# State-space decays through DRAM and GpSimd, unread bf16 products on TensorE, experts by pairs: one change to a twelve-stage kernel

## What is computed

```python
z, xs, Braw, Craw, dt_raw = split(layernorm(x) @ W_in)      # 512, 512, 64, 64, 64
dt = softplus(dt_raw + dt_bias)                             # 64 heads
a = exp(-exp(A_log) * dt)
Bh, Ch = rms(Braw) + B_bias, rms(Craw) + C_bias             # per head
phi = cumsum(dt, over tokens)[..., None] * rope_freqs
Bh, Ch = rope(Bh, phi), rope(Ch, phi)                       # r1 = v1*cos - v2*sin, r2 = v1*sin + v2*cos
h_t = a_t * h_(t-1) + (xs_t * dt_t) outer Bh_t ;  y_t = h_t . Ch_t
y = y / 8 + D_param * xs ;  g = y * silu(z) ;  x += (rms(g) * norm_w) @ W_out
```

## Time and profile before

| | us |
|---|---|
| median of three runs | 3548.45 (3546.27 to 3550.61) |
| the profiled execution | 3546.08 |
| its span, first to last instruction | 3543.8 |
| TensorE, matmul busy | 2886.8 (81%) |
| DVE busy | 2235.7 (63%) |
| ACT busy | 1481.2 (42%) |
| POOL busy | 628.6 (18%) |
| mean granted TensorE clock | 0.879 of 2.4 GHz |
| state-space stage, its first to its last instruction | 1030.7 to 1520.0 |
| expert stage | 2083 to 2307.5 |

### The profile page before, as it was taken

One profiled execution on the slowest core, in us unless ns is written; L12 is line 12 of the kernel. 1 busy time (PEld: TensorE's weight loads), 2 busy tenths in 40 slices (PEclk: granted clock), 3 DMA queues, 4 the chain that ended last, 5 costly groups with the idle time before them and its releaser, 6 DMA issues. The chain is left out here.

```text
span 3543.8 us, 63690 instructions
## 1 busy us (share of the span) xinstructions
PE 2886.8 (81%) x24052; PEld 2012.8 (57%) x24052; DVE 2235.7 (63%) x4757; ACT 1481.2 (42%) x3064; POOL 628.6 (18%) x990
## 2 busy tenths in 40 slices
PE   6777699977767878848996958979999996888687
PEld 3333488867645555525664434536565565777576
DVE  6999644432658888866655733257777774433764
ACT  4899511111454646343442122245555541332222
POOL 5222100000002222111110014112222212322100
PEclk8899799989977776769998978989999997999798
DMA  4999900000010000010001050000000003000000
GB/s 122 199 204 205 225 4 0 0 24 3 17 54 3 3 2 3 2 73 10 6 12 50 23 143 24 0 7 4 3 3 3 3 3 148 1 1 1 1 1 13
DMA packets 316791, 141.92 MB, mean 40 GB/s; under 512 B 296251, under 2 KB 306107, under 8 KB 312897
## 3 DMA queue, kind: packets, MB, share of 16 engines
q1 hardware_dynamic: 308356, 138.85, 16.4%
q10 hardware_dynamic: 8256, 0.52, 0.2%
HBM read 68.04 MB, written 3.15 MB: 20 GB/s over the span
## 5 line engine op out<-in xcount | busy, mean ns | idle before, releaser
L1251 ACT ACTIVATE l0x_pb<-l0x_ex,l0x_neg_max,l0x_q_scale 128x2048 uint16<-128x2048 f32 x128 | 267.2, 2088 | 35.3 <-POOL l0x_neg_max L1354 24.8
L1150 PE MATMUL l0x_s_ps<-l0x_kT,l0x_qT 128*128 128x512 bf16 x512 | 178.3, 440 | 78.8 <-DVE l0x_ex L1449 42.1
L1447 DVE TENSOR_SCALAR_CACHE_REDUCE l0x_ex<-l0x_s_ps 128x1024 f32<-128x1024 f32 x128 | 156.1, 1220 | 13.6 <-PE l0x_s_ps L1150 12.8
L1449 DVE TENSOR_SCALAR_CACHE_REDUCE l0x_ex<-l0x_s_ps 128x1024 f32<-128x1024 f32 x128 | 156.1, 1219 | 1.0 <-PE l0x_s_ps L1150 1.0
L1150 PEld LDWEIGHTS l0x_s_ps<-l0x_kT,l0x_qT 128*128 128x128 bf16 x512 | 33.5, 101 | 157.7 <-DVE l0x_ex L1449 106.3
L264 PE MATMUL l3x_bank<-l3x_w_kv_x,l3x_ctxT 128*128 128x512 f32 x256 | 117.4, 601 | 4.4 <-ACT l3x_ctx_q L765 3.7
L2230 PE MATMUL l1a_bank<-l1a_r,l1a_r 32*64 32x64 f32 x2048 | 73.1, 285 | 44.6 <-DVE l1a_r L2572 40.1
L2238 PEld LDWEIGHTS l1a_bank<-l1a_u,l1a_gm 64*64 64x64 f32 x2048 | 97.7, 197 | 17.8 <-issue 17.0
L2238 PE MATMUL l1a_bank<-l1a_u,l1a_gm 64*64 64x8 f32 x2048 | 100.4, 237 | 7.5 <-DVE l1a_gm L2591 7.3
L264 PE MATMUL l2f_bank<-l2f_w,l2f_ln_yT 128*128 128x352 f32 x256 | 105.6, 548 | 0.0
L1160 PEld LDWEIGHTS l0x_o_ps<-l0x_v,l0x_vT 128*128 128x128 f16 x2048 | 71.6, 99 | 56.5 <-DMA l0x_vT<-l0x_pb 26.7
(11 more groups left out here) (775 smaller groups left out, 7690.5 us busy)
## 6 DMA issues: line engine op xcount, KB each, us to landing
l2f_wproj_raw<-in_L_xattn_wproj SPq DMA_DIRECT2D x2, 2048.0 KB, 13.4
l3a_w<-in_L_attn_W SPq DMA_DIRECT2D x4, 1024.0 KB, 11.8
l2f_w<-in_L_ffn_w SPq DMA_DIRECT2D x1, 2816.0 KB, 10.7
l0x_ex<-in_ctxT SPq DMA_DIRECT2D x8, 256.0 KB, 5.3
l0a_wq<-in_L_attn_W_Q SPq DMA_DIRECT2D x1, 2048.0 KB, 11.4
l0a_wk<-in_L_attn_W_K SPq DMA_DIRECT2D x1, 2048.0 KB, 14.2
l0x_vT<-l0x_pb SPq DMA_TRANSPOSE x128, 4.7
l0a_wv<-in_L_attn_W_V SPq DMA_DIRECT2D x1, 2048.0 KB, 8.0
```

What stands on the lines that cost most here:

```text
L1150: ins = mm(s_ps[:, j * 512:(j + 1) * 512], qT[:, h, :], kT[:, h // 2, j * 512:(j + 1) * 512], start=True, stop=True)
L1251: s.activation(pb[:, h % 4, :], ex[:, h % 4, :], ACT.Exp, scale=q_scale[:, h:h + 1], bias=nb[:, h:h + 1], accum_out=sums[:, h:h + 1]).then ...
L1447: v.tensor_scalar(ex[:, h % 4, 0:1024], s_ps[:, 0:1024], 1.0, None, ALU.mult, ALU.max, accum_out=low_max[:, h:h + 1]).then_inc(o.up(scores ...
L1449: v.tensor_scalar(ex[:, h % 4, 1024:2048], s_ps[:, 1024:2048], 1.0, None, ALU.mult, ALU.max, accum_out=high_max[:, h:h + 1]).then_inc(o.up ...
```

## The change

In `l1_attn` the `differences` of TensorE, both kinds of steps and `dta` go. The running sum times `-exp(A_log)` is taken by ACT from the PSUM bank (`cum_a`, heads on partitions), stored to DRAM by SP and read back eight times per tile with the source repeated over 64 partitions, straight into `decay`. TensorE transposes `cum_a` to tokens on partitions (`cum_s`). POOL subtracts and adds the mask, for 16 heads at a time; ACT's exponential then works in place. `biased_b` is POOL's alone, in halves; `biased_c` and `sines` go by halves. `keep_warm` issues bf16 products of 128 x 512 whose result nobody reads. Per tile there are 22 while the next half is turned, 16 in `group_scores`, 11 in `mix`. In `Moe` two experts (2 x 176 = 352 = 128 + 128 + 96 columns) share three transposes, three products and two copies.

```diff
 class Moe:
-        self.parts = [(a, min(P, inner - a)) for a in range(0, inner, P)]
+        self.parts = [(a, min(P, 2 * inner - a)) for a in range(0, 2 * inner, P)]
...
-            if 1 <= i <= E:
+            if i >= 2 and i % 2 == 0:
...
-            if i >= 2:
+            if i >= 3 and i % 2:
...
+                s.activation(flat(self.actT[:, pair % 2, 0:whole_rows, :]), self.tb[:, 0:whole_rows * P], ACT.Copy)
@@ l1_attn, sync
+            for t in range(TILES):
+                sp.wait_ge(cum_a_ready.sem, cum_a_ready.value(t))
+                sp.dma_start(cum_dram[t].rearrange("b h s -> h b s"), cum_a[0:H, :].rearrange("h (b s) -> h b s", b=2)).then_inc(cum_stored.sem, 16)
+                sp.wait_ge(cum_stored.sem, cum_stored.value(t))
+                for r in range(4):
+                    if t and r % 2 == 0:
+                        sp.wait_ge(gm_ready.sem, gm_ready.value(t - 1, r // 2 + 1))
+                    for b in range(2):
+                        src = cum_dram[t, b, 16 * r:16 * r + 16, :].unsqueeze(0).broadcast_to([S, 16, S])
+                        sp.dma_start(decay[b * S:(b + 1) * S, 16 * r:16 * r + 16, :], src).then_inc(spread_loaded[r].sem, 16)
@@ l1_attn, tensor
-            def differences(t, r):
...
+            def keep_warm(n, spare):
...
+                for _ in range(n):
+                    mm(spare[:], warm[:, 0:P], warm[:], start=True, stop=True)
             def group_scores(half, lo=0, hi=8):
                 for j in range(lo, hi):
+                    keep_warm(1, bank[4])
...
                 for h in range(lo, hi):
+                    if h % 6 == 0:
+                        keep_warm(1, spare)
...
+            def turn_sums(t):
+                pe.wait_ge(cum_a_ready.sem, cum_a_ready.value(t))
...
+                nc.tensor.transpose(cum_s_bank, cum_a[0:H, :], env.ident[0:H, 0:H]).then_inc(cum_s_ps.sem, 1)
...
             def tile(t, more):
-                pe.wait_ge(exp_ready.sem, exp_ready.value(t, 1))
-                differences(t, 1)
+                pe.wait_ge(frac_ready.sem, frac_ready.value(t))
...
+                keep_warm(6, bank[4])
+                for k in range(2):
+                    pe.wait_ge(turning.sem, turning.value(t, k + 1))
...
+                    keep_warm(8, bank[4])
...
-                for r in range(2, 4):
-                    pe.wait_ge(exp_ready.sem, exp_ready.value(t, r))
-                    differences(t, r)
...
-                mix(30, 40)
+                mix(30, 40, bank[0])
                 if more:
+                    turn_sums(t + 1)
                     angles(t + 1)
...
-                if more:
-                    first_differences(t + 1)
@@ l1_attn, scalar
+                s.activation(cum_a[:], bank[2][:, 256:384], ACT.Copy, scale=a_neg[:]).then_inc(o.up(cum_a_ready), 1)
                 s.activation(cum[:], bank[2][:, 256:384], ACT.Copy, scale=1.0 / TWO_PI).then_inc(o.up(cum_ready), 1)
...
+                    act.wait_ge(roped.sem, roped.value(t, 1))
+                    biased_c(o, 0)
+                    sums_out(o)
+                    sines(o, 0)
                     act.wait_ge(roped.sem, roped.value(t))
-                    biased_c(o)
-                    sines(o)
+                    biased_c(o, 1)
+                    sines(o, 1)
@@ l1_attn, gpsimd
-            def odd_steps_of(o, r):
...
+            def differences(o, r):
...
+                heads = slice(16 * r, 16 * r + 16)
+                d = decay[:, heads, :]
+                pool.wait_ge(spread_loaded[r].sem, spread_loaded[r].value(o.t))
+                pool.wait_ge(cum_s_ready.sem, cum_s_ready.value(o.t))
+                g_.tensor_tensor(d, d, cum_s[:, heads].unsqueeze(2).broadcast_to([P, 16, S]), ALU.subtract).then_inc(o.up(), 1)
+                pool.wait_ge(o.sem, o.at())
+                g_.tensor_tensor(d, d, mask[:].unsqueeze(1).broadcast_to([P, 16, S]), ALU.add).then_inc(o.up(diff_ready), 1)
...
             def tile(t, more):
...
-                odd_steps_of(o, 3)
+                differences(o, 2)
+                differences(o, 3)
...
-                    odd_steps_of(o, 1)
-                    biased_b(o)
+                    for half in range(2):
+                        biased_b(o, half)
+                    differences(o, 0)
+                    differences(o, 1)
@@ l1_attn, vector
-                v.tensor_tensor(dta[:], dt[:, 0, :], a_neg[:], ALU.mult).then_inc(o.up(dt_ready), 1)
...
-                steps_of(o, 2)
...
-                    steps_of(o, 0)
-                    biased_b(o)
                     fractions(o)
```

More of the change, by code:

```diff
@@ L2379, in z_out @@
+                s.activation(d, d, ACT.Exp).then_inc(o.up(exp_ready), 1)
             def z_out(o):
@@ L2456, in _ @@
             first = Order(pool, L.sem("pool_first_order"))
             norms(first)
-            pool.wait_ge(dt_ready.sem, dt_ready.value(0))
-            odd_steps_of(first, 1)
-            biased_b(first)
+            pool.wait_ge(mask_set.sem, mask_set.value())
+            for half in range(2):
+                biased_b(first, half)
+            for r in range(2):
+                differences(first, r)
             def tile(t, more):
@@ L2470, in tile @@
                     scales_of_states(o)
-                    pool.wait_ge(dt_ready.sem, dt_ready.value(t + 1))
-                    odd_steps_of(o, 1)
-                    biased_b(o)
+                    for half in range(2):
+                        biased_b(o, half)
+                    differences(o, 0)
+                    differences(o, 1)
                     o.t = t
```

210 lines of the change are left out of this document (99 added, 111 removed).

## The result

The changed kernel takes **3640.39 us** (median of 4 runs, 3635.39 to 3643.43), the kernel before 3547.36 in the same comparison (3545.91 to 3550.61): a ratio of 1.026, 95% interval 1.0242 to 1.0277. It is slower by 93 us. The forecast was 3597, in a range that holds the result, and slower had the chance of 0.78. Rival (a), the half clock, gave 3633. In what follows the dense products are the unread bf16 products of 128 x 512 that `keep_warm` issues, and the small ones are those of `group_scores` and `mix`.

The account below looks back on a forecast made before the run. The prediction took a nearly full DVE (53.3 of 61 us) to bound the state-space stage. 3546.1 + 68 (state space) - 19 (experts) = 3595.1, put at 3597 us as that execution lies 2.4 under the median; range 3535 to 3650.

Parts of the forecast that it names:

- Rival (a): State-space stage: clock stays at 1.2 GHz in `group_scores(1)` and `mix`; +13 us per tile, about 3633 us; chance 0.24.
- POOL's collisions: State-space tile: POOL's eight new instructions hold up DVE's two-SBUF-input multiplies, +4.7 us at the start and +7.5 in `begin`.
- second burst: POOL's four instructions for rounds 0 and 1 of the next tile, released before `begin`: +7.5 us per tile.
- hand-over: POOL and DVE changing hands: the skill's 115 ns would add 0.9 us per tile; the sum left it out.
- The clock: TensorE in `group_scores` and `mix`: dense products bring the full clock, more likely than not; `group_scores(1)` 5.0 us, level with 4.8.
- share of 0.22 in `mix`: Dense products' share of time in `mix`, under the 0.38 that held clock 1.00 in the first stage.
- price of a dense product: TensorE: each dense product costs 0.22 us at the full clock, twice that at half.
- DVE's removed work: Between `weigh(1)` and `begin`: less DVE work and an earlier sine give -3.5 us per tile, 1.6 of it the sine.
- The sum: State-space tile: 58.4 + 4.7 + 7.5 - 3.5 - 0.2 = 66.9 us, +8.5 per tile; stage +68 us.
- Loads: Store and eight 256 KB loads, 2.7 us each, serial, some 24 us from the running sum; bounds 0 and 3 per tile.
- Experts: Expert stage: pairs save 0.69 us each, 32 pairs, less 0.7 per loop end: -19 us, bounds -12 and -24.
- Rival (c): Expert stage: no gain, because the wait for a whole pair's copies shows on TensorE; 3616 us; chance 0.07.

Follow-up runs that it names:

- e2: Changed kernel with POOL's subtraction and mask addition done on one head in sixteen, the rest left out: 3563.20 us.
- e8: Changed kernel without dense products, with eight no-work DVE instructions and POOL's subtraction and mask on one head in sixteen in all four rounds: 3476.45 us.
- e11: Changed kernel without dense products, with eight no-work DVE instructions and POOL's subtraction and mask on one head in sixteen in rounds 2 and 3 only: 3517.49 us.
- e5: Changed kernel without dense products and with eight no-work semaphore increments on DVE's queue in the state-space set-up: 3576.51 us.
- e12: Changed kernel with TensorE's idle wait before the first `group_scores` filled whole, 40 unread products behind the states' projection and 8 later: 3644.06 us.
- e9: Changed kernel with TensorE's idle wait filled (38 more unread products per tile) and two dense products for each one in `group_scores` and `mix`: 3626.95 us.
- e1: Changed kernel without any of its dense products: 3588.78 us.
- e7: Changed kernel with TensorE's idle wait filled (38 more unread products per tile) and four dense products for each one in `group_scores` and `mix`: 3656.68 us, one run.

## Why the prediction was right or wrong

**The direction was right, the range held, and the likeliest case was not what happened.** By its steps:

*POOL's collisions* were the forecast's reason for slower, and e2, e8 and e11 show them. At the tile's start it forecast +4.7 and got 14.07 - 8.84 = 5.2. In `begin` it forecast +7.5 and got +1.9 in the changed kernel and +3.6 in e5. To these come 0.8 and 1.5 us ahead of `begin`, where POOL holds DVE's multiply by `silu_z` (e2, and e8 against e5), so the second burst costs 2.6 and 5.1. The term was mis-sized, since in the changed kernel three of POOL's four instructions were over when `begin` started and only the last met DVE there. The hand-over stands as rows 4 had it: POOL's 3.21 us are its own 2.04 and DVE's 1.14, which leaves 0.03 us for the change of hands, so it was right to give that no price of its own in the sum.

*The clock* is the step that failed: "I take the full clock, more likely than not." It stood at 0.50 from `mix(0, 18)` into `begin` with the products in. Rival (a) put that at +13 per tile and 3633 us; it was 15.4 and 3640. That the totals are so near is in part luck: the stage came out 20 us above rival (a), the experts 24 below, and 16 came in stages that no case had. The forecast also left out TensorE's wait of 11.26 us ahead of `mix(0, 18)`, which the removed differences open and in which the clock falls. The reason given for rival (a), the share of 0.22 in `mix`, is not borne out: in e12 `mix(0, 18)` runs at 1.00 with it, until the next wait. And the price of a dense product was too low: 0.22 us at the full clock and twice that at half, where the rows show 0.32 and 0.54. `group_scores(1)` with the products took 9.2 us at 0.50 and not 8.3, and at 1.00 it would have been about 6.1, as `group_scores(0)` is, and not 5.0. Part of this lies in the record counts of the windows, which include records begun before the window and so make a small record look shorter than by its starts. So even the full clock would not have made this part level (0.79 against 0.71 us per group).

*DVE's removed work* was forecast at -3.5 us per tile between w(1) and `begin`. In e5 that stretch is 8.64 + 5.30 + 3.22 = 17.2 us against 16.6, so nothing was gained. Two things took it: the angles come from TensorE at half clock (e9, at the full clock, has them 1.6 us earlier), and POOL holds DVE for 1.5 us ahead of `begin`. In e8, with POOL out of the way, `begin` starts 1.3 us sooner after `g` than before, the sine, and the stretch is 15.6. This term too hung on the clock.

*The sum hid this.* e5 comes at 67.2 us per tile and 562 for the stage, where 66.9 and 561 were forecast, but by +5.2, -0.5, +0.5 and +3.6 in place of +4.7, 0, -3.5 and +7.5. It is the forecast's number for a kernel without dense products, and by chance.

*Loads*: the forecast took them for serial, some 24 us from the running sum. They overlap, and the last is there after 15.2, one about every 1.1 us. POOL waited once, 1.0 us in the tile read, where no wait was forecast. The bound of 3 us per tile held.

*Experts*: -43 instead of -19, outside the bounds of -12 and -24. The term was mis-sized in its price: all products of w2 were put at 1.15 / 4 = 0.29 us, but those of 128 rows take 0.22 and the 48-row ones carry the two stops. By the starts of a pair in one tile it is 5.32 us before and 4.02 after, 1.30 less and not 0.69. Rival (c) fell: TensorE waited 1.2 us in all for the copies.

*Another stage* was not in the forecast at all: 10 us from eight instructions less.

## What to carry to other kernels

Before you buy clock with unread products, work out from one group's rows what the group takes at both clocks: in `group_scores` 0.24 us was on offer and one product cost 0.32, in `mix` 0.58 was on offer for the same 0.32. Work handed to POOL is paid by DVE wherever both use SBUF operands, so count it by what DVE does at the moment of release, and expect it to cost more once other waits are gone. A part of 48 rows among parts of 128 costs more than its rows; fill it up or pair it.

## What the runs showed of the hardware that was not expected

- In `group_scores(1)` with one dense product to 32 small ones the granted clock stayed at 0.50 while TensorE was busy for 2.00 of every 2 us (e12); with two it came back to 1.00 (e9), with none it did so in some tiles (e1), and with four and no wait over 0.47 us it didn't fall (e7). In `group_scores(0)` it was at 1.00 with one, in half of the changed kernel's tiles. The runs give no account that fits all of these.
- A change between 128-row and 48-row weights stopped the loads for 0.33 us each time; 96 rows showed no stop.
- Eight instructions less on DVE made a loop of the same queue, in a stage far behind the edit, 10 us longer, and eight of no work undid it.
- Eight loads of 256 KB issued within 4.9 us landed one about every 1.1 us, the last 12 us after the first issue, with a median of 5.8 us from issue to landing; eight others, each alone, took 2.7.
